# A transposed copy of x as a further input, queries of 448 columns, and the high and low part of x made by GpSimd

## What is computed

```python
x = x + attention(layernorm(x), ctx_512, Wq, Wkv_expand, Wout)
x = x + ffn(layernorm(x), ...)

def layernorm(x):
    m = mean(x); v = var(x)
    return (x - m) / sqrt(v + 1e-5)

def attention(q, latent_kv, Wq, Wkv, Wout):
    qp = q @ Wq.T                                   # 512 -> 512
    k, v = split(latent_kv @ Wkv.T)                 # 128 -> 2 x 512
    scores = qh @ kh / sqrt(32)                     # 16 heads
    scores = where(causal, scores, finfo.min)
    return softmax(scores) @ vh @ Wout.T
```

## Time and profile before

| | |
|---|---|
| median of 3 runs (lowest, highest) | 1526.69 us (1522.23, 1528.37) |
| the profiled execution: its own time, span of its trace | 1524.8 us, 1523.0 us |
| granted TensorE clock, mean of the execution | 0.998 |
| busy: PE, DVE, ACT, POOL | 98%, 57%, 40%, 38% of the span |
| 100 to 150 us (steady steps): PE, DVE, ACT, POOL | 49.97, 35.17, 39.07, 15.69 of 50 us |

### The profile page before, as it was taken

The page is one execution under the profiler, slowest core; times in us unless marked ns, Lnnn a source line. Parts: engine busy times, 40 slices in busy tenths (PEclk is TensorE's granted clock), DMA queues, the critical chain, the costliest instruction groups (busy, mean ns, idle before and its releaser), DMA issues.

```text
span 1523.0 us, 29819 instructions
## 1 busy us (share of the span) xinstructions
PE 1492.7 (98%) x10482; PEld 1279.4 (84%) x10482; DVE 869.7 (57%) x1490; ACT 611.8 (40%) x1836; POOL 580.9 (38%) x502
## 2 busy tenths in 40 slices
PE   6999999999999999999999999999999999999999
PEld 5788888888877899999999999887888888888887
DVE  6667677777665577877867867455223322233322
ACT  5877777777754333323333333422111111111111
POOL 3333446555553277865865965112100001000010
PEclk9999999999999999999999999999999999999999
DMA  6133354434356589877778765553303012030110
GB/s 193 56 99 99 86 106 87 87 91 99 75 128 123 104 317 340 287 245 266 274 257 275 248 217 184 203 183 103 98 27 111 28 54 70 14 111 28 58 54 28
DMA packets 98287, 209.96 MB, mean 138 GB/s; under 512 B 43184, under 2 KB 44208, under 8 KB 93456
## 3 DMA queue, kind: packets, MB, share of 16 engines
q1 hardware_dynamic: 86576, 177.37, 37.9%
q0 software_dynamic: 11616, 31.35, 7.2%
HBM read 161.52 MB, written 47.17 MB: 137 GB/s over the span
## 4 chain that ended last, share of the span: by engine, by line
PE 88%; DVE 3%; DMA 3%; ACT 2%; issue 2%; POOL 1%; SPq 0%; POOLq 0%; DVEq 0%; ACTq 0%
PE psum L802 62%; PE psum L1126 11%; PE psum L936 3%; PE psum L927 2%; PE psum L1028 2%; ACT probs L1227 2%; PE psum L955 1%; PE psum L1052 1%; PE psum L964 1%; PE psum L993 1%; PE psum L887 1%; PE psum L944 1%; DMA wj_raw<-in_w_shared 1%; PE psum L918 1%; PE psum L815 1%
## 5 line engine op out<-in xcount | busy, mean ns | idle before, releaser
L1527 POOL DMA_INDIRECT routed<-expert_out_dram,slot_b x56 | 55.6, 993 | 479.1 <-DVE slot_b L1986 289.3
L2004 DVE TENSOR_TENSOR h_s<-psum,silu_s 128x512 f32<-128x512 f32 x66 | 45.7, 692 | 299.6 <-PE psum L802 295.2
L802 PE MATMUL psum<-nT_hi,ws_hi 128*128 128x512 f32 x528 | 208.8, 396 | 2.9 <-DVE nT_lo L1927 2.6
L802 PE MATMUL psum<-nT_lo,ws_hi 128*128 128x512 f32 x528 | 208.6, 395 | 0.0
L802 PE MATMUL psum<-nT_hi,ws_lo 128*128 128x512 f32 x528 | 208.6, 395 | 0.0
L1227 ACT ACTIVATE probs<-psum,minus_max 112x112 f32<-112x112 f32 x512 | 176.2, 430 | 3.4 <-DVE minus_max L1662 3.4
L1499 POOL DMA_INDIRECT xg<-normed_dram,tile_ids x63 | 149.9, 2379 | 37.5 <-DMA tile_ids<-lists_dram 18.6
L802 PE MATMUL psum<-wj_hi,gT_hi 128*128 128x352 f32 x504 | 162.8, 323 | 0.0
L802 PE MATMUL psum<-wj_hi,gT_lo 128*128 128x352 f32 x504 | 162.3, 322 | 0.0
L802 PE MATMUL psum<-wj_lo,gT_hi 128*128 128x352 f32 x504 | 161.8, 321 | 0.0
L1227 ACT ACTIVATION_READ_ACCUMULATOR probs<-psum,minus_max 112x1 f32 x512 | 145.3, 284 | 0.0
(11 more groups left out here) (244 smaller groups left out, 3585.3 us busy)
## 6 DMA issues: line engine op xcount, KB each, us to landing
wj_raw<-in_w_experts SPq DMA_DIRECT2D x35, 1408.0 KB, 6.5
wj_raw<-in_w_experts SPq DMA_DIRECT2D x35, 768.0 KB, 5.2
wj_raw<-in_w_shared SPq DMA_DIRECT2D x22, 768.0 KB, 5.3
expert_out_dram<-y_c SPq DMA_DIRECT2D x63, 256.0 KB
base<-x_dram SPq DMA_DIRECT2D x8, 1024.0 KB, 5.9
x_in<-in_x SPq DMA_DIRECT2D x32, 224.0 KB, 4.1
x_res<-in_x SPq DMA_DIRECT2D x32, 224.0 KB, 3.1
x_dram<-x SPq DMA_DIRECT2D x32, 224.0 KB, 3.8
```

What stands on the lines that cost most here:

```text
L802: mm = pe.matmul(out_ap, u, v, start=(n == 0), stop=(n == last))
L1527: pool.indirect_dma_start(out=routed[:, b % 2, c, :], out_offset=None, in_=expert_out_dram, in_offset=bass.IndirectOffsetOnAxis(ap=slot_b[ ...
L2004: dve.tensor_tensor(h_s[:, :], bank(b), silu_s[:, :], ALU.mult).then_inc(emptied_b[b], 1)
```

## The change

- A copy of x that is transposed on the host (`xT`, channels on the partitions) is a further input. SP loads it per entry into `xT_raw` (224 KB), eight entries ahead.
- The high and low part of the transposed x are made from the raw x: for entries 0 to 7 by ScalarE (`x_hi`) and VectorE (`x_lo`) ahead of the steps, for the others by GpSimd in the loop (`split_x`), both into one of two buffers of a whole group.
- The layernorm is applied elsewhere. The mean is taken out of Wq once at the start: TensorE multiplies Wq by a matrix of 1/512 in float32 (`weight_means`), and VectorE subtracts it (`centre`). The factor 1/sqrt(v + eps), with the 1/sqrt(32) of the scores in it, is given to the exponential as a scale per row (`rs1`) in place of a constant, and to `minus_max`. `norm1`, `rows_across` and the PSUM turns `x0` and `xT` go.
- Each step makes one row block m = j of the queries for the whole next group: 12 matmuls of 448 columns. For the first group the old form of 224 columns remains, two at the start and two (`q0`, 2 and 3) in steps 0 and 1. `qT` has two buffers.
- All steps are written out; the hardware loop goes.

```diff
+            def weight_means():
+                pe.wait_ge(S["mean_step"], 1)
+                pe.wait_ge(w_loaded[1], 16)
                 for k in range(KC):
+                    mm = pe.matmul(bank(0), mean_f[:, :], wq_raw[:, k, :], start=(k == 0), stop=(k == KC - 1))
+                mm.then_inc(S["mean_step"], 1)
...
             def next_front(g, j):
                 at, to = half_of(j)
+                if is_first(g) and j < 2:
+                    pe.wait_ge(S["xT_split"], TB)
+                    queries(take(0, j, "q0", 2 + j), 0, HALVES[j], HT, GT)
+                if there(g, j, -TB):
+                    pe.wait_ge(S["xT_split"], TB * (g + 2))
+                    queries(take(g, j, "q"), g + 1, (j,), 0, GT)
                 if there(g, j, -2):
-                    queries(take(g, j, "q"), HALVES[j % 2], at, to)
                     pe.wait_ge(S["ctx_split"], halves_split(g, j))
                     keys(take(g, j, "k"), HALVES[j % 2], at, to)
-                if there(g, j, -TB):
-                    pe.wait_ge(S["xn1_ready"], g * TB + j + TB + 1)
-                    rows_across(take(g, j, "xT"), j)
...
                                     done = act.activation(probs[:, j % 2, 4 * r + m, :], psum[0:SEQ, r, m * SEQ:(m + 1) * SEQ], ACT.Exp,
-                                                          bias=minus_max[:, r, m:m + 1], scale=SCALE,
+                                                          bias=minus_max[:, r, m:m + 1], scale=rs1[:, j % 2, 1:2],
                                                           accum_out=rsum[:, j % 2, 4 * m + r:4 * m + r + 1])
...
+            def split_x(t):
+                cols = slice(t % TB * SEQ, (t % TB + 1) * SEQ)
+                hi, lo = xT_hi[t // TB % 2][:, :, cols], xT_lo[t // TB % 2][:, :, cols]
+                pool.wait_ge(S["xT_hi_made"], t)
+                pool.wait_ge(xT_loaded[t % TB], 16 * (t // TB + 1))
+                settled(pool)
+                pool.tensor_scalar(hi, xT_raw[:, t % TB, :, :], 1.0, 0.0, ALU.mult, ALU.add).then_inc(S["xT_hi_made"], 1)
+                pool.wait_ge(S["xT_hi_made"], t + 1)
+                pool.tensor_tensor(lo, xT_raw[:, t % TB, :, :], hi.bitcast(F32), ALU.subtract).then_inc(S["xT_split"], 1)
...
-                    if before(g, NG - 1):
-                        inverse_root(mv1, rs1, j % 2, "stats1", "rstd1_made", t + TB + 1)
+                    if there(g, j, -1):
+                        scaled_root(t + 1)
+                    if there(g, j, -2 * TB):
+                        split_x(t + 2 * TB)
...
+            x_lo(0)
+            x_lo(1)
             weights_lo(0)
+            centre(0)
+            centre(1)
             weights_lo(1)
             weights_lo(2)
             mask_copies()
-            stats1(2, 3, 1)
-            stats1(3, 4, 1)
-            norm1(2, 3)
-            norm1(3, 4)
+            stats1(0)
+            x_lo(2)
+            x_lo(3)
             weights_lo(3)
-            for n in range(2, 4):
-                x_lo(0, -1, "x0", n, n)
+            for t in range(TB, 2 * TB):
+                x_lo(t)
...
+                    dve.wait_ge(S["rstd1_made"], 2 * (t + 1))
                     dve.wait_ge(S["scores_done"], t + 1)
```

More of the change, by code:

```diff
@@ L79, in nth, with build_program @@
     def nth(self, g, j, stage, part=0):
-        if stage not in ("x0", "q0", "k0") and j < 0:
+        if stage not in ("k0", "q0") and j < 0:
             g, j = g - 1, j + TB
         b = self.bank(stage, part)
[L84 to L87, removed]
+        return sum(len(self.of(i, b)) for i in range(g)) + self.of(g, b).index((j, stage, part)) + 1
     def bank(self, stage, part=0):
         return next(bank for key, _, bank in TURNS if key[1:] == (stage, part))
-def build_program(nc, x, ctxT, wq, wkv, wout, gates, w_experts, w_shared, out):
+def build_program(nc, x, xT, ctxT, wq, wkv, wout, gates, w_experts, w_shared, out):
     NB = x.shape[0]
@@ L488, in wait_emptied, with groups @@
             eng.wait_ge(emptied[turns.bank(stage, part)], nth(g, j, stage, part))
[L490 to L497, removed]
+        def groups(body):
+            for g in range(NG + 2):
                 body(g)
@@ L612, in body @@
                         tail_loads(g, j)
[L613 to L616, removed]
+                    if there(g, j, -2 * TB):
+                        load_xT(t + 2 * TB)
+                    if there(g, j, -TB):
+                        load_x(t + TB)
                 if routes(g):
@@ L1008, in _ @@
             pe.wait_ge(S["consts_made"], 2)
-            groups(pe, body, 1)
+            groups(body)
             for c in TAIL_CHUNKS:
@@ L1144, in weights_hi, with x_hi @@
                 raw, hi, _ = SPLITS[n][1:]
-                act.wait_ge(w_loaded[SPLITS[n][0]], 16)
+                if SPLITS[n][0] == 1:
+                    act.wait_ge(S["wq_centred"], n)
+                else:
+                    act.wait_ge(w_loaded[SPLITS[n][0]], 16)
                 act.activation(hi, raw, ACT.Copy).then_inc(S["w_hi_made"], 1)
[L1148 to L1152, removed]
+            def x_hi(t):
+                cols = slice(t % TB * SEQ, (t % TB + 1) * SEQ)
+                act.wait_ge(xT_loaded[t % TB], 16 * (t // TB + 1))
+                act.activation(xT_hi[t // TB % 2][:, :, cols], xT_raw[:, t % TB, :, :], ACT.Copy).then_inc(S["xT_hi_made"], 1)
             def evacuate(g, j, stage, part, dst, ms, at, to):
@@ L1670, in step @@
                     n0_low(3)
-                if before(g, NG - 1) and not (is_first(g) and j == 0):
-                    stats1(j, t + TB + 1, g + 2)
+                if there(g, j, -1):
+                    stats1(t + 1)
                 if not is_late(g, 0):
                     rows_copy(g, j)
-                if before(g, NG - 1):
-                    if is_first(g):
-                        wait_filled(dve, 0, -1, "x0", j)
-                    else:
-                        wait_filled(dve, g - 1, j, "xT")
-                    norm1(j, t + TB + 1)
                 if there(g, j, 1):
@@ L1884, in body @@
                             table_second()
-            groups(dve, body, 2)
+            groups(body)
             def tokens_lo(q, k):
```

191 lines of the change are left out of this document (98 added, 93 removed).

## The result

The changed kernel takes 1683.45 us (median of 4 runs, 1682.83 to 1684.43), the kernel before in the same runs 1527.06 us. The ratio is 1.1031, with a 95% interval of 1.1006 to 1.1056: 10.3% slower, where no change was forecast.

A forecast was written before the change was run, and what follows sets the result against it. TensorE's work was taken to bound plain steps, with a VectorE-ScalarE-GpSimd chain as near from the third group on. Terms 6 - 3.5 - 2.6 - 3.5 + 1.3 + 4 = +1.7 on 1524.8 gave about 1527 us, range 1510 to 1538.

The forecast's parts named there:

- The failed step: GpSimd's splits and SP's extra 224 KB load a step: covered, by 1 us, a cost of nothing.
- Exponentials: ScalarE, first stage: the scale operand per row adds 0.08 us to each of 16 exponentials, 1.3 us a step.
- TensorE: the queries: First stage: queries take 2.49 us, 0.27 saved; with row transposes gone, 0.59 us saved a step.
- A group with choices: Groups 2 to 6, first stage: four steps take 54.1 us instead of 52.9, +1.2 each, +6 in all.
- Start: Before the steps: first maxima at 27.2 instead of 24.49 us; +4 with the longer exponentials.
- steps 3 to 8: Early first-stage steps without choices keep slack in the chain: six times -0.59, -3.5 us.
- step 26 itself: Group 6: VectorE's late addition, TensorE's 1.22 us wait and the low clock after it; counted as -2.6 us.
- the steps to 30: Steps 28 and 29, without queries, bound by exponentials: about 11.2 instead of 13.0 us, -3.5 together.
- The scale costs nothing: Rival, exponentials on ScalarE: both operands are read together, -15, about 1512 us; chance 0.30.
- GpSimd is late because the splits are held: Rival, GpSimd: splits take 3 to 4 us, five groups lose 1 to 1.5 each, about 1533 us; chance 0.07.
- The waits let the clock fall: Rival, TensorE: waits before `normT` halve its clock, six of ten give +10, about 1537 us; chance 0.17.
- The change does less than it says: Rival, first stage: scores still wait, as `x_in` of the next step comes late; chance 0.03.

The follow-up runs named there:

- the waits filled: Changed kernel with 8 matmuls before TensorE's wait for the spread inverse sums and 7 before that for the second rows, steps 3 to 23: 1655.44 us, ratio 1.0836.
- the load at the head: Changed kernel with the load of entry t+8 as the first thing in SyncE's step t, not at its end: 1525.72 us, ratio 0.9971.
- the runs without and with the operand: Changed kernel, loads three steps earlier: exponential's scale as the old constant, 1509.56 us, or as the operand per row, 1532.79 us.
- only the first wait filled: Changed kernel with 8 matmuls of 512 columns before TensorE's wait for the spread inverse sums, steps 3 to 23: 1663.28 us, ratio 1.0874.
- the swap: GpSimd makes second rows before spreading inverse sums: changed kernel, loads three steps earlier, 1521.87 us; load first in SyncE's step, 1524.36; kernel before, 1528.85.

## Why the prediction was wrong

**The failed step** stands in the part on GpSimd: "SP gets one load of 224 KB more a step, well ahead. A cost of nothing". "Well ahead" was taken from the entry's number, t+8 in step t. What counts is the distance between the place of the load in SyncE's program and the place of the wait in GpSimd's, and both are in step t: the load at its end, behind a wait for the projection of step t, the split ahead of what the projection of step t+1 needs. The part named what the 1.8 us of splits push back, but not what is queued behind the *wait* in the split, which is all of GpSimd. In place of "a cost of nothing" the runs show 156 us. One step more between load and split, at either end, brings 1683 to 1526 or 1531 us; a ring shorter by 3.8 us (the load ahead of four transfers) brings it to 1577.

**The size** follows from the ring. From the end of one projection (204.72) to the spread inverse sums (214.84) it is 10.1 us; root and second rows take 3.6 more (to 218.44), transposes 0.4 and projection 2.85 at full clock. That is 17.0 us; measured with the waits filled, 16.7. With issue and landing 1.9 us shorter each it would be 13.2; measured, 13.0. A free step takes 12.4 us. The scores of step 3 start at 59.77 and those of step 25 at 504.77; with the load at the head it is 59.78 and 352.83. The difference, 152 us in 22 steps, is nearly the whole loss, 6.9 us a step. With the waits filled (60.32 to 479.76) 126 of it remain, 5.7 a step: 4.3 for the plain ring (16.7 - 12.4), and the rest in the groups with choices. There, by the timeline, the late split pushes the scatters in front of the inverse sums (in the run with the load ahead of four transfers the split starts at 193.52, three scatters follow, and `rinv_wide` starts at 199.10); this part was read, not tested.

**The other steps** can be judged in the kernel with the load at the head, which is the change as the prediction took it to be. It lasts 1525.72 us beside 1528.88 of the kernel before: -0.3%, where 0.0% was forecast. (The forecast's own sum gives 1526.5 + 1.9 = 1528.4 rather than 1527; the slip is small.)

- Exponentials: 0.09 us each instead of 0.08. Right in the single price. What it adds up to was put at 15 us (1527 and 1512); the runs without and with the operand differ by 23.
- TensorE: the queries take 2.54 us (206.24 to 208.78 in the kernel after) for the forecast 2.49, no row transposes, plain steps of 12.40 us (85.77 to 98.17) for 12.4. Right.
- A group with choices: scores of 17, 19 and 21 at 242.79, 270.76 and 296.64, so 53.85 us for the forecast 54.1; 52.9 before. TensorE waits for `xn` in front of its transposes, as forecast:

```profile
242.79 1.05 PE L935 MATMUL psum<-kT,qT 32*112 32x112 f32 x32
...
261.71 0.60 PE L972 MATMUL psum<-ident,xn 112*128 112x112 f32 x4 [1.52 <-POOL xn L1472]
...
270.76 1.05 PE L935 MATMUL psum<-kT,qT 32*112 32x112 f32 x32
...
296.64 1.05 PE L935 MATMUL psum<-kT,qT 32*112 32x112 f32 x32
```

- Start: first maxima at 26.54 us instead of 24.49, forecast 27.2. Right in kind, 0.7 too much.
- Splits: 0.57 and 1.13 us, 1.70 in all for the forecast 1.8.
- The terms of the sum, read from the starts of the scores in the two traces: the start +3.1 (step 3 at 59.78 for 56.67) for the forecast 4; steps 3 to 8 -3.0 for -3.5; the groups with choices +6.4 (step 9 at 135.34 for 135.21, step 26 at 365.97 for 359.44) for 6; step 26 itself -2.0 for -2.6; the steps to 30 -3.6 for -3.5. The two traces are 1525.0 and 1523.0 us long, +2.0 for +1.7.

The agreement of the +6.4 is in part luck: 3.3 of it come from one step, 22, in which TensorE stopped between two matmuls with no releaser in the profile, and the granted clock behind the stop was 0.50. Its cause stays open.

```profile
316.03 0.39 PE L963 MATMUL psum<-probsT,v_sb 112*32 112x112 f32 x4 [1.97 <-issue]
...
318.00:320.00 2.00, 2.00 (x6) 1.49 (x5) 0.24 (x1) 2.00 (x12) 1.75 (x3) 0.50 0.00 0
```

**The rivals.** "The scale costs nothing" is refuted (0.42 against 0.33 us). "GpSimd is late because the splits are held" is refuted in its mechanism: the splits run at their own speed. But its sign, waits for `rinv_wide`, came in full, from another cause; a sign that two causes share had been given to the cheaper one. "The waits let the clock fall" is real but follows from the ring: with the ring open (the load at the head) the mean clock is 0.996 in spite of 16 waits of up to 1.7 us, in the kernel after it is 0.944. "The change does less than it says" has nothing for it: no wait of TensorE in the trace with the load at the head goes back to a late `x_in`. None of the four rivals was the load of `xT`.

## What to carry to other kernels

When a change adds a load and a consumer, write down for one step where the load stands in the issuing engine's program, behind which waits, and where its consumer stands, ahead of what. If the load waits for a piece of work of this step, and its consumer in this step stands ahead of what the same piece of work needs in the next one, it is a ring, whatever the prefetch distance in entries, and the step is at least the sum round it. Here the buffer slot had been free for more than three steps, and moving two lines took 158 us off. The Trainium skill (DMA: Bandwidth & Descriptors, section Rules for kernel authors) says to issue early and wait late. Here "early" had to be measured in waits of the issuing engine, not in entries.

Where an engine runs its program in order, as GpSimd does here, an added instruction holds up all that is queued behind it by its duration and by its wait: here 1.7 us and 11.5 us a step.

## What the runs showed that had not been expected

- The last of five transfers of 224 KB in SyncE's queue lands 4.7 us after its issue (median), the first of them 2.8 us. The last one had also been issued 1.9 us later, so its place in the burst counted twice, with about the same amount.
- With only the first wait filled, TensorE did 0.60 us of transposes and 0.97 us of attention output and then waited 1.79 us; the granted clock behind that was 0.50, though 8 matmuls of 512 columns stood ahead of it. With the 1.79 us filled too it stayed at 1.00 in the steps without choices. In the kernel with the load at the head, waits of up to 1.7 us at the same place were not followed by a fall (clock 1.00 from 50 to 300 us), and with the loads three steps earlier not even one of 2.10 us was. But with the load at the head and the swap, a wait of 1.71 us for the inverse sums (before 240.36) was followed by 0.50. So the length of the wait alone doesn't decide; what else does was not tested.
- Matmuls of 4 us a step, put in front of TensorE's waits, made the kernel 28 us *faster*.
